# Four partial-sum tables in two alternating scatter chains, joined by VectorE and TensorE, in an attention and mixture-of-experts kernel

## The chip, the cores and the metric

The kernel runs on one core of one Trainium2 chip. The metric is the device time of one execution in microseconds (us). Engines: TensorE (PE in the profile; PEld is its weight load), VectorE (DVE), ScalarE (ACT), GpSimd (POOL) and SyncE (SP), which here only issues DMA transfers.

## The reference

Four batches of 1024 tokens with 256 values each go through two residual blocks in float32. A is causal attention with 16 query heads of 128 and 4 key and value heads with rotary positions. F is a mixture of experts: sigmoid scores of 64 experts, the best 4 of 8 groups, the best 6 experts in them, weights normalized and times 2.5, at most 48 tokens per expert, each expert a gated layer of 96, and beside it one shared expert of the same shape.

```python
x = x + layernorm(A(layernorm(x)))
x = x + layernorm(F(layernorm(x)))
# F: y = segment_sum(out[expert, slot] * weight, token); return y + shared(x)
```

## The kernel before

`attention` runs from the start to about 1780 us and also does the routing of the first seven of eight groups of 512 tokens (a "quad"); `last_quad` does the last quad and the shared expert; `experts` (L1626 on) takes the experts in 32 pairs and then finishes the output. The change is mostly in `experts`.

**Tables.** The sum over the experts of a token is kept in HBM, in partial-sum tables of 4144 rows (4096 tokens and 48 rows for padding) of 1 KB. All three are parts of one tensor `sums`. The shared expert is written to table 0 beforehand and the others start at zero: `attention` writes zeros to table 1 and copies them to table 2 at its step 40 (L1096). GpSimd adds a pair's 128 result rows to the tables by an indirect DMA with addition (a "scatter"); the even expert's 64 rows and the odd expert's 64 rows go to different tables, because one token may be in both. An accumulating DMA reads and writes back, so two scatters that can touch one table must not be in flight together; each waits for the landing of the one before in its chain.

**The chains before.** `in_third_table(j)` is true for every third pair up to the 27th. The other pairs form chain 0 (`added[0]`, tables 0 and 1, 23 scatters). The nine third pairs form chain 1 (`added[1]`): both of their halves go to table 2, so each is two scatters (`scatter_half`, L1732), one for each expert of the pair, the other's rows being sent out of bounds.

**Turns.** TensorE runs 35 turns. Turn s transposes the gathered tokens of pair s (L1876), does gate and up of pair s-1 (L1888), transposes the hidden values of pair s-2 (L1896) and does down of pair s-3 (L1903). ScalarE copies and applies tanh, VectorE multiplies in `hidden(s-1)` and weights the odd expert's rows in `odd(s-3)` (L1779), after which the pair's scatter may be issued. GpSimd's queue is in order: the gather of pair j+6, then the scatter of pair j (and one half of a third pair). The ring of gathered pairs has eight places, the ring of results `y` four.

**The finish.** The 32 token tiles are taken in eight units of four tiles (128 x 1024 values, 512 KB). SyncE loads table 2 into `m2` (L1705) when chain 1 has landed, and tables 0 and 1 into `m0` and `m1` (L1711) when chain 0 has. Then, for each unit: GpSimd adds m2 to m0 (L1751), VectorE adds m1 (L1796), takes mean and variance (L1798, L1803), ScalarE the root (L1857), VectorE seven small operations for the reciprocal root with one Newton step and the shift (L1807 to L1813), ScalarE normalizes (L1866), and VectorE (L1792) or for three of the units GpSimd (L1756) adds the residual `x1`. SyncE stores the unit (L1715). The x1 rows, 4 MB, are loaded at the seventh pair (L1700).

## Time and profile before

| | |
|---|---|
| median of three runs | 2067.99 us (2067.24 to 2068.68) |
| the profiled execution's own time | 2069.03 us |
| its span, first to last instruction | 2067.2 us |
| busy: TensorE, VectorE, ScalarE, GpSimd | 1869.7, 1348.5, 1155.7, 1303.5 us |
| mean granted TensorE clock | 0.942 of 2.4 GHz |
| expert turns, first TensorE to last TensorE instruction | 1847.8 to about 1977.5 us |
| last scatter issued, landed | 1995.1, 1998.9 us |
| loads of tables 0 and 1 issued, first addition | from 1998.9, 2004.4 us |
| last residual addition begins | 2062.6 us |

Times within the trace are microseconds from the start of the span. A busy time counts an engine's instructions, not its waits or issues; what an engine waited for is inferred from semaphore events.

### The profile page before, as it was taken

The numbers are of one execution on the slowest core, as the hardware profiler recorded it, in microseconds if no ns is written. First come the engines' busy times: TensorE is split into PE (matmuls) and PEld (weight loads), VectorE is DVE, ScalarE is ACT, GpSimd is POOL, SyncE is SP. The second block draws the span as 40 slices with busy tenths as digits, with TensorE's granted clock in tenths as the row PEclk, the third lists the DMA queues.
The fourth block names the chain that finished last, engine by engine and source line by source line (L and its number), as shares of the span: only waits on it lengthen the run. The fifth ranks groups of instructions, "written<-read, shape, count | busy, mean of one in ns | idle before, by whom it ended". The sixth has DMA issues, their size and how long they took to land. (4 is left out here: it accounts for less than half of the span.)

```text
span 2067.2 us, 34272 instructions
## 1 busy us (share of the span) xinstructions
PE 1869.7 (90%) x11782; PEld 1554.9 (75%) x11782; DVE 1348.5 (65%) x3198; ACT 1155.7 (56%) x2632; POOL 1303.5 (63%) x1057
## 2 busy tenths in 40 slices
PE   5999999999999999999999999999999999776820
PEld 4888888888888888888888888888888887442310
DVE  5566666667767677767767667766676678641228
ACT  3656666666666655656666556566656555232313
POOL 5758575767766666767585758576666654226843
PEclk8999999999999999999999999999999999895555
DMA  5003000001110101000200000010001000586374
GB/s 179 14 26 104 6 22 6 22 6 32 47 52 6 42 6 27 2 26 32 67 12 16 32 6 27 6 52 27 32 6 42 14 4 27 218 322 198 58 201 143
DMA packets 74233, 111.77 MB, mean 54 GB/s; under 512 B 10790, under 2 KB 54772, under 8 KB 72928
## 3 DMA queue, kind: packets, MB, share of 16 engines
q1 hardware_dynamic: 61040, 88.42, 12.8%
q0 software_dynamic: 8544, 12.73, 2.7%
q10 hardware_dynamic: 4480, 8.44, 1.2%
q8 instruction: 97, 1.59, 0.3%
q14 instruction: 72, 0.59, 0.1%
HBM read 81.90 MB, written 35.47 MB: 57 GB/s over the span
## 5 line engine op out<-in xcount | busy, mean ns | idle before, releaser
L561 PE MATMUL s_ps<-kT,q 128*128 128x512 f32 (+3 forms) x2304 | 584.4, 372 | 13.9 <-POOL q L1135 7.7
L824 DVE TENSOR_TENSOR pT<-t_ps,pT 128x512 fp32r<-128x512 f32 (+3 forms) x768 | 401.2, 550 | 191.4 <-ACT pT L969 190.1
L811 DVE TENSOR_REDUCE neg_max<-s_ps 128x1 f32<-128x640 f32 (+7 forms) x512 | 384.9, 752 | 111.3 <-PE s_ps L561 104.4
L561 PEld LDWEIGHTS s_ps<-kT,q 128*128 128x128 f32 x2304 | 408.4, 192 | 61.7 <-ACT probs L958 11.6
L586 PE MATMUL av_ps<-pT,v 128*128 128x512 f32 x1728 | 442.5, 400 | 2.7 <-DVE pT L824 2.7
L1120 POOL TENSOR_TENSOR k_roped<-raw,sinT 64x512 f32<-64x512 f32 x316 | 407.3, 1289 | 24.3
L969 ACT ACTIVATE pT<-t_ps 128x512 fp32r<-128x512 f32 (+3 forms) x768 | 348.7, 490 | 130.2 <-PE t_ps L571 125.3
L958 ACT ACTIVATE probs<-s_ps,neg_max 128x640 f32<-128x640 f32 (+7 forms) x512 | 381.9, 746 | 63.4 <-DVE neg_max L811 61.1
L586 PEld LDWEIGHTS av_ps<-pT,v 128*128 128x128 f32 x1728 | 311.7, 189 | 67.5 <-DVE pT L824 7.8
L571 PE MATMUL t_ps<-k_ident,probs 128*128 128x128 f32 x2304 | 340.1, 274 | 11.6 <-DVE pT L824 5.9
L1117 POOL TENSOR_TENSOR k_roped<-raw,cosT 128x512 f32<-128x512 f32 x158 | 204.7, 1296 | 219.5 <-ACT raw L930 200.8
L571 PEld LDWEIGHTS t_ps<-k_ident,probs 128*128 128x128 f32 x2304 | 263.3, 140 | 37.3 <-ACT probs L958 12.7
L598 PE MATMUL misc_ps<-w_o,avT 128*128 128x256 f32 x1536 | 237.9, 290 | 15.5 <-DVE y L856 8.1
L598 PEld LDWEIGHTS misc_ps<-w_o,avT 128*128 128x128 f32 x1536 | 205.0, 189 | 33.4 <-ACT raw L930 12.9
L856 DVE SCALAR_TENSOR_TENSOR y<-misc_ps,inv_sum,y 128x256 f32<-128x256 f32 x448 | 215.0, 480 | 14.1 <-PE misc_ps L598 6.1
L1122 POOL TENSOR_TENSOR raw<-k_roped 128x512 f32<-128x512 f32 x158 | 202.9, 1284 | 12.4
L518 PE MATMUL misc_ps<-xT,w_q 128*128 128x256 f32 x1524 | 204.2, 283 | 1.8 <-DVE y L856 1.8
L518 PEld LDWEIGHTS misc_ps<-xT,w_q 128*128 128x128 f32 x1524 | 194.7, 190 | 3.7 <-DVE y L856 2.4
L829 DVE TENSOR_TENSOR avT<-av_ps,avT 128x512 fp32r<-128x512 f32 x128 | 88.6, 692 | 135.6 <-ACT avT L976 135.4
L976 ACT ACTIVATE avT<-av_ps 128x512 fp32r<-128x512 f32 x128 | 76.3, 596 | 161.1 <-PE av_ps L586 159.1
L939 ACT ACTIVATE q<-raw 128x512 fp32r<-128x512 f32 x128 | 80.6, 630 | 151.1 <-POOL raw L1122 151.1
L1135 POOL TENSOR_TENSOR q<-raw,q 128x512 fp32r<-128x512 f32 x128 | 163.5, 1291 | 1.8 <-ACT q L939 1.8
(234 smaller groups left out, 1871.1 us busy)
## 6 DMA issues: line engine op xcount, KB each, us to landing
w_early<-in_expert_w SPq DMA_DIRECT2D x5, 2560.0 KB, 26.7
k_staged<-in_wpack SPq DMA_DIRECT2D x47, 256.0 KB, 2.9
k_staged<-in_wpack SPq DMA_DIRECT2D x16, 512.0 KB, 3.6
w_early<-sums SPq DMA_DIRECT2D x16, 512.0 KB, 8.5
e_w_late<-in_expert_w SPq DMA_DIRECT2D x3, 2560.0 KB, 21.5
sums<-sums ACTq DMA_DIRECT2D x1, 4144.0 KB, 15.6
k_xw<-in_x SPq DMA_DIRECT2D x4, 1024.0 KB, 5.8
k_xb<-in_x SPq DMA_DIRECT2D x4, 1024.0 KB, 5.1
```

What stands on the lines that cost most here:

```text
L518: last = pe.matmul(bank("q", macro, half)[:, h * 256:(h + 1) * 256], w_q[:, s, half, c, h * HD:(h + 1) * HD], pair(xT[:, b % 2, a, c], m), ...
L561: last = pe.matmul(out, q[:, macro % 2, a, h, int(big)], kT[:, g % 2, s, lo:hi], start=(n == 0), stop=(n == 2))
L571: last = pe.transpose(t_ps[n % 2][:, j * P:(j + 1) * P], probs[:, r % 3, (first + j) * P:(first + j + 1) * P], ident[:])
L586: last = pe.matmul(av_ps[:], v[:, g % 2, a, j], pT[:, s, part_slot(p) + j], start=(j == 0 and n == 0), stop=(j == blocks - 1 and n == 2))
L598: last = pe.matmul(misc_ps[:, h * HID:(h + 1) * HID], avT[:, a, 2 * half + h], w_o[:, s, 2 * half + h], start=(n == 0), stop=(n == 2))
L811: dve.reduce_max(neg_max[:, r % 16:r % 16 + 1], s_ps[:, r % 2, 0:(row_tile(r) + 1) * P], AX.X, negate=True).then_inc(max_ready, 1)
L824: dve.tensor_tensor(lo, t_ps[n % 2][:, 0:count * P].rearrange("p (j n) -> p j n", n=P), hi.bitcast(F32), ALU.subtract).then_inc(t_lo, 1)
L856: last = dve.scalar_tensor_tensor(target[:, t], src, inv, y[:, t], ALU.mult, ALU.add)
L958: act.activation(probs[:, r % 3, 0:width], s_ps[:, r % 2, 0:width], ACT.Exp, bias=neg_max[:, r % 16:r % 16 + 1], accum_out=row_sum[:, r % ...
L969: act.activation(pT[:, 0, slot + first:slot + first + count, r % 4], t_ps[n % 2][:, 0:count * P].rearrange("p (j n) -> p j n", n=P), ACT.C ...
L1117: pool.tensor_tensor(shape(cosed), shape(raw[:, n % 2]), table(cosT, 0, P), ALU.mult).then_inc(cos_done, 1)
L1120: pool.tensor_tensor(shape(rope[64 - lo:128 - lo]), shape(raw[lo:hi, n % 2]), table(sinT, lo, hi), ALU.mult).then_inc(sin_done, 1)
```

## The change

There are four tables. For the first 28 pairs (`TURNS = 14`), even pairs go to chain 0 (tables 0 and 1) and odd pairs to chain 1 (tables 2 and 3), each pair as one scatter. The last four pairs all go to chain 0. `attention` copies zeros to table 3 as well. The index calculation in `last_quad` has six VectorE operations in place of ten.

Tables 2 and 3 are loaded (8 MB) when chain 1 has landed, into `m2` and `m3`. VectorE adds m3 to m2, two units in each of its turns s = 31 to 34, behind `hidden` and `odd` of the turn, waiting for the unit's loads. Tables 0 and 1 are loaded as before when chain 0 has landed, now into `m0` in the late weights' space and `m1`, which is m3's space, so each unit also waits for its joining.

In the finish GpSimd adds m2 to m0; TensorE then adds m0 and m1 by two float32 matmuls with the identity into each of two PSUM banks (four matmuls of 512 columns per unit); VectorE takes the statistics from PSUM, and ScalarE normalizes from PSUM into m0. The Newton step is gone: VectorE does one reciprocal, GpSimd the two small operations of the shift (`shift_of(u-1)`, queued behind its addition of unit u), and VectorE adds all residuals, that of unit u-1 queued between the statistics and the reciprocal of unit u.

Besides, some semaphores of `attention` are merged (`quad_mv`, `quad_rstd` in place of one for each of y and x1; `zeroed` becomes a link of the chain), with the same order of work, and SyncE waits at the end of `attention` for both zero copies. The diff without these, and without declarations:

```diff
@@ attention, last_quad @@
-                    act.dma_start(sums[2], sums[1]).then_inc(zeros_copied, 16)
+                    for n in (2, 3):
+                        act.dma_start(sums[n], sums[1]).then_inc(zeros_copied, 16)
...
-TURNS = 9
-
-
-def in_third_table(j):
-    return j % 3 == 2 and j < 3 * TURNS
+TURNS = 14
+
+
+def in_second(j):
+    return j % 2 == 1 and j < 2 * TURNS
 
 
 def scattered_earlier(j):
-    return sum((1 + in_third_table(i)) for i in range(j) if in_third_table(i) == in_third_table(j))
+    return sum(in_second(i) == in_second(j) for i in range(j))
...
-            third = slice(2, 3 * TURNS, 3)
+            second, first = slice(1, 2 * TURNS, 2), (slice(0, 2 * TURNS, 2), slice(2 * TURNS, EXPERTS // 2))
             for i in range(2):
-                half, other = slice(64 * i, 64 * i + 64), slice(64 - 64 * i, 128 - 64 * i)
-                target = index.to_third[:] if i else index.to_row[:, third]
-                dve.tensor_scalar(target[half], c_ps[1][half, third], -1.0, FAR + 2 * TABLE, ALU.mult, ALU.add).then_inc(index_done, 1)
-                dve.tensor_scalar(target[other], c_ps[1][other, third], 0.0, 2 * FAR, ALU.mult, ALU.add).then_inc(index_done, 1)
-                for cols in (slice(0, 3 * TURNS, 3), slice(1, 3 * TURNS, 3), slice(3 * TURNS, EXPERTS // 2)):
-                    dve.tensor_scalar(index.to_row[half, cols], c_ps[1][half, cols], -1.0, FAR + i * TABLE, ALU.mult, ALU.add).then_inc(index_done, 1)
+                half = slice(64 * i, 64 * i + 64)
+                for cols, table in ((second, 2 + i), (first[0], i), (first[1], i)):
+                    dve.tensor_scalar(index.to_row[half, cols], c_ps[1][half, cols], -1.0, FAR + table * TABLE, ALU.mult, ALU.add).then_inc(index_done, 1)
...
@@ experts @@
+        sum_ps = [t_ps, gu_ps, hT_ps, y_ps]
+
+        def summed_tile(u, t):
+            return sum_ps[u % 4][t // 2][:, (t % 2) * HID:(t % 2) * HID + HID]
...
-        x1, m2, m0 = (flat[:, i * SIZE:(i + 1) * SIZE].rearrange("p (t n) -> p t n", n=HID) for i in range(3))
-        m1 = w_late[:].rearrange("p e n -> p (e n)")[:, 0:SIZE].rearrange("p (t n) -> p t n", n=HID)
+        x1, m2, m3 = (flat[:, i * SIZE:(i + 1) * SIZE].rearrange("p (t n) -> p t n", n=HID) for i in range(3))
+        m0, m1 = w_late[:].rearrange("p e n -> p (e n)")[:, 0:SIZE].rearrange("p (t n) -> p t n", n=HID), m3
...
-            sp.wait_ge(y_ready, last_pair(1))
-            sp.wait_ge(added[1], 32 * TURNS)
+            sp.wait_ge(y_ready, last_pair(2))
+            sp.wait_ge(added[1], 16 * TURNS)
             for u in range(UNITS):
-                first = 2 * TABLE + u * UNIT * P
-                sp.dma_start(unit(m2, u), tiles(sums[first:first + UNIT * P])).then_inc(loaded[u], 16)
+                first = u * UNIT * P
+                for dst, table in ((m2, 2 * TABLE), (m3, 3 * TABLE)):
+                    sp.dma_start(unit(dst, u), tiles(sums[table + first:table + first + UNIT * P])).then_inc(loaded[u], 16)
             sp.wait_ge(y_ready, PAIRS)
             sp.wait_ge(added[0], 16 * (PAIRS - TURNS))
             for u in range(UNITS):
                 first = u * UNIT * P
+                sp.wait_ge(joined, u + 1)
                 for dst, table in ((m0, 0), (m1, TABLE)):
...
-                if in_third_table(j):
-                    scatter_half(j, 0)
-                else:
-                    scatter(j)
-                if j and in_third_table(j - 1):
-                    scatter_half(j - 1, 1)
+                pool.wait_ge(y_odd, j + 1)
+                if scattered_earlier(j):
+                    pool.wait_ge(added[in_second(j)], 16 * scattered_earlier(j))
+                pool.indirect_dma_start(sums, bass.IndirectOffsetOnAxis(to_row[:, j:j + 1], 0), y[:, j % Y_RING], None,
+                                        bounds_check=4 * TABLE - 1, oob_is_err=False, compute_op=ALU.add).then_inc(added[in_second(j)], 16)
+            link = Links(pool, pool_chain, 0, 0)
+
+            def shift_of(u):
+                pool.wait_ge(rstd_ready, u + 1)
+                if u >= 2:
+                    pool.wait_ge(normed, u - 1)
+                link(pool.tensor_tensor(centre[:, u % 2], mv[:, u % 2, :, 0], rstd[:, u % 2], ALU.mult))
+                pool.tensor_tensor(shift[:, u % 2], kept.shift[:, u * UNIT:(u + 1) * UNIT], centre[:, u % 2], ALU.subtract).then_inc(shift_ready, 1)
+
             for u in range(UNITS):
-                pool.wait_ge(loaded[u], 48)
-                pool.tensor_tensor(unit(m0, u), unit(m0, u), unit(m2, u), ALU.add).then_inc(summed, 1)
-                if u >= 2 and on_pool(u - 2):
-                    if u == 3:
-                        pool.wait_ge(x1_in, 16)
-                    pool.wait_ge(normed, u - 1)
-                    pool.tensor_tensor(unit(m0, u - 2), unit(m0, u - 2), unit(x1, u - 2), ALU.add).then_inc(done[1], 1)
-            for n, count in enumerate((PAIRS - TURNS, 2 * TURNS)):
+                pool.wait_ge(loaded[u], 64)
+                pool.tensor_tensor(unit(m0, u), unit(m0, u), unit(m2, u), ALU.add).then_inc(padded, 1)
+                if u:
+                    shift_of(u - 1)
+            shift_of(UNITS - 1)
+            for n, count in enumerate((PAIRS - TURNS, TURNS)):
...
+                first = 2 * (s - (PAIRS + 3 - UNITS // 2))
+                for u in range(max(first, 0), first + 2):
+                    dve.wait_ge(loaded[u], 32)
+                    dve.tensor_tensor(unit(m2, u), unit(m2, u), unit(m3, u), ALU.add).then_inc(joined, 1)
...
-                link(dve.tensor_tensor(unit(m0, u), unit(m0, u), unit(m1, u), ALU.add))
+                if u >= 2:
+                    dve.wait_ge(mv_ready, u - 1)
+                    dve.wait_ge(shift_ready, u - 1)
                 for t in range(UNIT):
-                    last = dve.bn_stats(stats[:, t], m0[:, u * UNIT + t])
+                    last = dve.bn_stats(stats[:, u % 2, t], summed_tile(u, t))
                 link(last)
-                if u >= 2:
-                    dve.wait_ge(normed, u - 1)
                 for t in range(UNIT):
-                    last = dve.bn_aggr(mv[:, u % 2, t], stats[:, t])
-                last.then_inc(var_ready, 1)
+                    last = dve.bn_aggr(mv[:, u % 2, t], stats[:, u % 2, t])
+                last.then_inc(mv_ready, 1)
+                if u:
+                    residual(u - 1)
                 dve.wait_ge(root_done, u + 1)
-                mean, var, r = mv[:, u % 2, :, 0], mv[:, u % 2, :, 1], rstd[:, u % 2]
-                link(dve.reciprocal(r, root[:, u % 2]))
-                link(dve.tensor_tensor(newton[:], r, r, ALU.mult))
-                link(dve.scalar_tensor_tensor(newton[:], var, EPS, newton[:], ALU.add, ALU.mult))
-                link(dve.tensor_scalar(newton[:], newton[:], -0.5, 1.5, ALU.mult, ALU.add))
-                link(dve.tensor_tensor(r, r, newton[:], ALU.mult))
-                link(dve.scalar_tensor_tensor(shift[:, u % 2], mean, -1.0, r, ALU.mult, ALU.mult))
-                dve.tensor_tensor(shift[:, u % 2], shift[:, u % 2], kept.shift[:, u * UNIT:(u + 1) * UNIT], ALU.add).then_inc(rstd_ready, 1)
-                if u and not on_pool(u - 1):
-                    residual(u - 1)
+                dve.reciprocal(rstd[:, u % 2], root[:, u % 2]).then_inc(rstd_ready, 1)
             residual(UNITS - 1)
...
-                act.wait_ge(rstd_ready, u + 1)
+                act.wait_ge(shift_ready, u + 1)
                 for t in range(UNIT):
-                    at = m0[:, u * UNIT + t]
-                    last = act.activation(at, at, ACT.Identity, bias=shift[:, u % 2, t:t + 1], scale=rstd[:, u % 2, t:t + 1])
+                    last = act.activation(m0[:, u * UNIT + t], summed_tile(u, t), ACT.Identity, bias=shift[:, u % 2, t:t + 1], scale=rstd[:, u % 2, t:t + 1])
...
+            for u in range(UNITS):
+                pe.wait_ge(padded, u + 1)
+                if u >= 4:
+                    pe.wait_ge(normed, u - 3)
+                for k in range(2):
+                    bank = sum_ps[u % 4][k][:]
+                    for n, table in enumerate((m0, m1)):
+                        half = unit(table, u)[:, 2 * k:2 * k + 2].rearrange("p t n -> p (t n)")
+                        last = pe.matmul(bank, ident[:], half, start=(n == 0), stop=(n == 1))
+                last.then_inc(summed, 1)
+
```

## Rows read from the trace of the kernel before

**Rows 1.** GpSimd's timeline, steady turns: start, length, instruction, idle before it and releaser.
```profile
1927.37 1.59 POOL L1724 DMA_INDIRECT sums<-k_xb,i_to_row  x1 [0.30 <-issue]
...
1931.14 1.08 POOL L1741 DMA_INDIRECT i_gathered<-rows,i_from_row  x1 [0.30 <-issue]
...
1939.07 1.59 POOL L1724 DMA_INDIRECT sums<-k_xb,i_to_row  x1 [0.30 <-issue]
```

**Rows 2.** TensorE's timeline: starts of turns 15, 23, 24 and 28.
```profile
1905.96 0.69 PE L1876 MATMUL e_t_ps<-k_ident,i_gathered 128*128 128x128 f32 x2
...
1937.61 0.69 PE L1876 MATMUL e_t_ps<-k_ident,i_gathered 128*128 128x128 f32 x2
...
1941.14 0.69 PE L1876 MATMUL e_t_ps<-k_ident,i_gathered 128*128 128x128 f32 x2
...
1957.52 0.44 PE L1876 MATMUL e_t_ps<-k_ident,i_gathered 128*128 128x128 f32 x2 [1.67 <-DMA i_gathered<-rows,i_from_row]
```

**Rows 3.** The chain that ended last, first scatters: start, us from issue to landing.
```profile
1856.59 8.17 DMA sums<-k_xb,i_to_row
...
1865.62 7.04 DMA sums<-k_xb,i_to_row
...
1885.22 11.45 DMA sums<-k_xb,i_to_row
```

**Rows 4.** The same chain, from the 28th pair's scatter to the final loads.
```profile
1972.22 3.59 DMA sums<-k_xb,i_to_row
...
1976.62 5.16 DMA sums<-k_xb,i_to_row
...
1982.59 7.26 DMA sums<-k_xb,i_to_row
...
1990.66 3.67 DMA sums<-k_xb,i_to_row
...
1998.92 0.36 SPq L1711
```

**Rows 5.** Windows, the final loads: us, busy time by engine, granted clock, DMA share, GB/s.
```profile
2001.00:2026.00 25.00, 0.00 (x0) 0.00 (x0) 17.45 (x44) 5.04 (x11) 13.03 (x6) 0.50 1.09 352
```

**Rows 6.** Timeline of the finish.
```profile
2004.44 2.33 POOL L1751 TENSOR_TENSOR w_early<-w_early 128x1024 f32<-128x1024 f32 x1 [7.73 <-DMA e_w_late<-sums]
...
2010.46 2.34 DVE L1808 TENSOR_TENSOR e_newton<-e_rstd 128x4 f32<-128x4 f32 x1
...
2056.94 1.41 DVE L1798 BATCH_NORM_STATS2 e_stats<-w_early 128x6 f32<-128x256 f32 x4
...
2059.12 0.18 DVE L1807 RECIPROCAL e_rstd<-e_root 128x4 f32<-128x4 f32 x1 [0.36 <-ACT e_root L1857]
...
2060.52 2.07 ACT L1866 ACTIVATE w_early<-w_early,e_shift,e_rstd 128x256 f32<-128x256 f32 x4 [1.43 <-DVE e_shift L1813]
2062.63 1.23 DVE L1792 TENSOR_TENSOR w_early<-w_early 128x1024 f32<-128x1024 f32 x1 [1.01 <-ACT w_early L1866]
```

**Rows 7.** GpSimd's timeline: a small operation in `last_quad`.
```profile
1792.90 0.20 POOL L244 TENSOR_TENSOR k_work<-k_x_mv,k_x_rstd 128x4 f32<-128x4 f32 x1
```

**Rows 8.** One line's instructions, `odd`: count, shortest, median, longest ns.
```profile
L1779 DVE TENSOR_SCALAR k_xb<-e_y_ps,i_gathered x32: 488/490/493, 1855.3 to 1978.7; 64x256 f32<-64x256 f32 x32
```

**Rows 9.** TensorE's timeline, shared expert: two float32 matmuls of 512 columns each row.
```profile
1781.54 3.32 PE L1357 MATMUL r_gate<-k_staged,k_roped 128*96 128x512 f32 x4 [1.96 <-PEq L290]
...
1805.59 1.88 PE L1357 MATMUL r_gate<-r_xs,k_roped 128*96 128x512 f32 x4
1807.31 1.88 PE L1357 MATMUL r_up<-r_xs,k_roped 128*96 128x512 f32 x4
```

**Rows 10.** Windows of TensorE: us, busy, granted clock, DMA share, GB/s.
```profile
1784.00:1785.00 1.00, 1.00 (x3) 0.83 1.00 401
...
1958.00:1960.00 2.00, 2.00 (x13) 0.61 0.69 109
```

**Rows 11.** One line's instructions, the first gate matmuls, two records per matmul.
```profile
L1357 PE MATMUL r_gate<-k_staged,k_roped x4: 684/1061/1137, 1781.5 to 1784.2; 128*96 128x512 f32 x4
```

More of the change, by code:

```diff
@@ L357, in attention @@
         passed, copied, weight_done, weight_out = sem("passed"), sem("copied"), sem("weight_done"), sem("weight_out")
-        y_mv, x1_mv, x_mv, y_rstd, x1_rstd, x_rstd = (sem(n) for n in ("y_mv", "x1_mv", "x_mv", "y_rstd", "x1_rstd", "x_rstd"))
+        quad_mv, x_mv, quad_rstd, x_rstd = (sem(n) for n in ("quad_mv", "x_mv", "quad_rstd", "x_rstd"))
         score_done, biased_done, penalty_done, masked, picked_done, product_done, total_done = (
@@ L472, in _ @@
             sp.wait_ge(weight_out, 32 * (QUADS - 2))
-            sp.wait_ge(zeros_copied, 16)
+            sp.wait_ge(zeros_copied, 32)
         @block.tensor
@@ L696, in quad_stats @@
                 b, half = divmod(n, 2)
-                src, mv, mv_done, read = (xw, kept.y_mv, y_mv, y_rstd) if kind == "y" else (xb, kept.x1_mv, x1_mv, x1_rstd)
+                src, mv, turn = (xw, kept.y_mv, 2 * n) if kind == "y" else (xb, kept.x1_mv, 2 * n + 1)
                 if i == 0:
@@ L709, in quad_stats @@
                 else:
-                    if n:
-                        dve.wait_ge(read, n)
+                    if turn >= 2:
+                        dve.wait_ge(quad_rstd, turn - 1)
                     for k in range(4):
                         last = dve.bn_aggr(mv[:, k], kept.stats[:, k])
-                    last.then_inc(mv_done, 1)
+                    last.then_inc(quad_mv, 1)
             def add_residual(n, i):
                 if i == 0:
-                    dve.wait_ge(y_rstd, n + 1)
+                    dve.wait_ge(quad_rstd, 2 * n + 1)
                     dve.wait_ge(xb_in, 16 * (n // 2 + 1))
@@ L1658, in experts @@
         hT_ready, hT_read = sem("hT_ready"), sem("hT_read")
-        y_ready, y_even, y_odd = sem("y_ready"), sem("y_even"), sem("y_odd")
-        added = [sem(f"added{n}") for n in range(2)]
+        y_ready, y_even, y_odd, padded = sem("y_ready"), sem("y_even"), sem("y_odd"), sem("padded")
+        added, joined = [sem(f"added{n}") for n in range(2)], sem("joined")
         x1_in = sem("x1_in")
         loaded = [sem(f"loaded{u}") for u in range(UNITS)]
-        summed, var_ready, root_done, rstd_ready = (sem(n) for n in ("summed", "var_ready", "root_done", "rstd_ready"))
-        normed, done, stored = sem("normed"), [sem(f"done{n}") for n in range(2)], sem("stored")
+        summed, mv_ready, root_done, rstd_ready, shift_ready = (sem(n) for n in ("summed", "mv_ready", "root_done", "rstd_ready", "shift_ready"))
+        normed, done, stored = sem("normed"), sem("done"), sem("stored")
+        pool_chain = sem("pool_chain")
+        sum_ps = [t_ps, gu_ps, hT_ps, y_ps]
+        def summed_tile(u, t):
+            return sum_ps[u % 4][t // 2][:, (t % 2) * HID:(t % 2) * HID + HID]
         block = ctx.enter_context(nc.Block())
@@ L1676, in landed @@
         def landed(j):
-            return added[in_third_table(j)], 16 * (scattered_earlier(j) + 1 + in_third_table(j))
+            return added[in_second(j)], 16 * (scattered_earlier(j) + 1)
         def weights(e):
@@ L1686, in unit @@
             return a[:, u * UNIT:(u + 1) * UNIT]
-        def on_pool(u):
-            return u % 2 == 1 and u + 1 < UNITS
-        def finished(u):
-            return done[on_pool(u)], sum(on_pool(i) == on_pool(u) for i in range(u + 1))
         @block.sync
@@ L1712, in _ @@
             for u in range(UNITS):
-                sp.wait_ge(*finished(u))
+                sp.wait_ge(done, u + 1)
                 b, t = divmod(u * UNIT, NT)
@@ L1719, in _ @@
         def _(pool):
-            def scatter(j):
-                pool.wait_ge(y_odd, j + 1)
-                if j:
-                    pool.wait_ge(added[0], 16 * scattered_earlier(j))
-                pool.indirect_dma_start(sums, bass.IndirectOffsetOnAxis(to_row[:, j:j + 1], 0), y[:, j % Y_RING], None,
-                                        bounds_check=3 * TABLE - 1, oob_is_err=False, compute_op=ALU.add).then_inc(added[0], 16)
-            def scatter_half(j, i):
-                to = index.to_third[:, j // 3:j // 3 + 1] if i else to_row[:, j:j + 1]
-                pool.wait_ge(y_odd, j + 1)
-                if scattered_earlier(j) + i:
-                    pool.wait_ge(added[1], 16 * (scattered_earlier(j) + i))
-                pool.indirect_dma_start(sums, bass.IndirectOffsetOnAxis(to, 0), y[:, j % Y_RING], None,
-                                        bounds_check=3 * TABLE - 1, oob_is_err=False, compute_op=ALU.add).then_inc(added[1], 16)
             for j in range(PAIRS):
@@ L1855, in root_of @@
             def root_of(u):
-                act.wait_ge(var_ready, u + 1)
+                act.wait_ge(mv_ready, u + 1)
+                if u >= 2:
+                    act.wait_ge(rstd_ready, u - 1)
                 act.activation(root[:, u % 2], mv[:, u % 2, :, 1], ACT.Sqrt, bias=eps[:]).then_inc(root_done, 1)
@@ L1926, in build @@
         shared_in = ctx.enter_context(nc.semaphore("shared_in"))
-        attention(nc, args, x, wpack, x1_rows, rows, [sums[n * TABLE:(n + 1) * TABLE] for n in range(3)], x2t_rows, kept, shared_in)
+        attention(nc, args, x, wpack, x1_rows, rows, [sums[n * TABLE:(n + 1) * TABLE] for n in range(4)], x2t_rows, kept, shared_in)
         index = Index(lambda name, shape, dt=F32: ctx.enter_context(nc.sbuf_tensor("i_" + name, shape, dt)))
```

26 lines of the change are left out of this document (12 added, 14 removed).

## The prediction

> **What bounds the kernel now.** I read the page first. TensorE is busy 1869.7 of 2067.2 us, but that is attention, where the change adds only zero copies. So the question is the last 220 us, for which I read the chain that ended last, then the timelines of GpSimd and TensorE there, and the windows. Three stretches have three different limits.
>
> *The turns, 1848 to 1972.* In the steady part GpSimd never waits: between instructions it idles only 0.30 us of its own issue time. Two scatters three pairs apart start at 1927.37 and 1939.07, so three pairs take 11.70 us. That is four scatters (a third pair needs two) of 1.59 + 0.30 and three gathers of 1.08 + 0.30, or 3.90 us per pair [rows 1]. TensorE needs less: two turns without a wait start 3.53 us apart at the half clock (1.2 GHz) [rows 2]. Before 1900 the limit is different: scatters of chain 0 take 8.17, 7.04 and 11.45 us to land beside the loads of expert weights and of x1 [rows 3], and the in-order GpSimd queue, gathers included, stands behind them.
>
> *The tail, 1972.2 to 1998.9.* The 28th pair's scatter is issued at 1972.22, the four others follow each other's landings in chain 0, and the final loads are issued at 1998.92, which is 26.7 us later. Alone a scatter lands in 3.6 to 3.7 us, beside the table 2 loads in 5.16 and 7.26, and 0.8 us lie between a landing and the next issue [rows 4].
>
> *The finish, 1998.9 to 2067.2, 68.3 us.* GpSimd starts its first addition 5.5 us after the first load is issued. The loads run at 352 GB/s with the DMA share full [rows 5], so 1 MB of a unit takes 3.0 us, but units leave only every 7.3 us: the last VectorE operations begin at 2062.63 after eight units from 2004.44 [rows 6]. VectorE holds the chain. An operation on 128x4 values that elsewhere takes 0.16 to 0.20 takes 2.34 us when it lies under a GpSimd addition of the same length [rows 6, 7].
>
> **Part 1, one scatter per pair and four tables.** In the turns GpSimd then has one scatter and one gather, 1.89 + 1.38 = 3.27 us per pair, below TensorE's 3.53. So TensorE at the half clock becomes the limit, with no waits to hide: 3.54 us per pair, 0.36 less than before. The bound below is 3.27, if the clock rises in part. A chain has 7.1 us between its issues, more than the 3.7 of a landing, so it never holds the queue there.
>
> The start changes more. With two chains the second scatter no longer waits for the first to land: it goes at about 1859.9 in place of 1865.6, the eighth gather after it at 1861.8 in place of 1867.5. Carrying this forward pair by pair with the landings of [rows 3] (8 us beside the weights, 4 us between as alone, 11 beside x1, whose load also moves 4 us earlier) I get gathers at 1867.5, 1870.8, 1875.3, 1878.6, 1881.9, 1886.9 and 1894, and turn 15 begins at about 1898.1 in place of 1905.96 [rows 2], 7.9 us early. The 28th pair is done in turn 30: 1898.1 + 15 x 3.54 = 1951.2 is its start, + 3.54 for the turn, + 1.2 for ScalarE's and VectorE's halves and the issue, gives its scatter at 1956.2 to 1956.5. Before it was 1972.2: **-15.7 us**. The bounds are 1954 (GpSimd's pace) and 1960 (half the start's gain lost).
>
> **Part 2, the tail with 8 MB of loads and the joins.** It costs. Call the issue of the 8 MB L'; it follows the landing of the 28th pair, 3.8 us after its scatter. Loaded units come at L' + 5.5 and then every 3.0, the last at L' + 26.5, and nearly every scatter of the tail lies beside them. VectorE's queue is in order, so the joins also hold `hidden` and `odd` of the next turns, and for these TensorE and the scatters wait. The scatter of the 29th pair goes at L' - 0.3 and lands at L' + 7. Joins of units 0 and 1 end at L' + 9.7 (the unit at 8.5, a VectorE addition 1.2 [rows 6]); then the 30th pair's results and scatter at L' + 11, landed at 18.3 by the 7.26 of [rows 4]; the 31st at 19, landed at 26.3; the 32nd at 27, landed at L' + 30.8, where the loads are over. The joins are done by L' + 27.7, so the chain ends last. The final loads start 3.8 + 30.9 = 34.7 us after the 28th pair's scatter in place of 26.7: **+8.0 us**. With 5.2 per landing it would be L' + 28; with the 11.45 of the x1 load instead of 7.26 L' + 35: -3 and +4 us.
>
> **Part 3, the finish.** The final loads are again 8 MB, so the first addition is again 5.5 us after their issue and the padded unit 2.34 later. Per unit VectorE loses one addition (1.2), the Newton step and the slow small operations; TensorE gets four float32 matmuls of 512 columns. No such sum stands in the trace; nearest are the shared expert's gate and up, two such matmuls each: 1.72 us start to start at the full clock, 3.3 at the half one [rows 9]. So 3.44 or 6.7 us per unit. GpSimd's two small operations take 0.2 each [rows 7], statistics from PSUM 1.41 to 1.9 (between the 1.41 from SBUF [rows 6] and the 0.49 per tile of `odd`, which reads PSUM [rows 8]; I take 1.5, since it is the same operation).
>
> What limits is a loop: addition of unit u, TensorE's sum, statistics and aggregate, residual u-1, reciprocal, shift of u, and only then GpSimd adds unit u+2. At the full clock this is 2.34 + 3.7 for the sum with its last record's length + 1.9 for statistics and aggregate (the reciprocal starts 2.2 after the statistics, with ScalarE's root between [rows 6]) + 1.2 + 0.2 + 0.8 for the shift with its waits, 10.2 us for two units, 5.1 per unit. The first unit is padded 7.85 after the issue, the second 3.0 later, the eighth 3 x 10.2 after the second and 2.4 more for a first sum at the half clock, its sum 3.7 later: 39.7 after the first. The last statistics, residual of unit 7, reciprocal, shift, normalizing (2.07) and residual (1.2) are 1.9 + 1.2 + 0.2 + 0.8 + 2.1 + 1.2 and some waits, 7.6; store and end, as before, 3.3. Together 58.5 us.
>
> The clock. TensorE is cold before it. It rose 2.8 us after the first of the 512-column matmuls (1781.54, window 1784 to 1785) [rows 9, 10], so it will rise in the first unit; in the loop TensorE then idles 1.6 us in each 5.1. In the turns the clock fell within 2.5 us after an idle of 1.67 us (turn 28, window 1958 to 1960) [rows 2, 10], though smaller matmuls surrounded it. I therefore add 2 us for partial falls: 60.5 in place of 68.3, **-7.8 us**. Always cold, TensorE alone takes 8 x 6.9 (6.7 and a wait) = 55 us after the first padded unit: 7.85 + 55 + 7.6 + 3.3 = 73.8, or +5.5.
>
> The Trainium skill, page "TensorE: Matmul & The Clock Gate", section "A second HAM failure mode: psum-queue depth-cycling", describes a kernel whose TensorE idles briefly between groups of matmuls while it cycles PSUM banks, often enough that its clock keeps going back and forth. By that rule the finish would lie between my two cases; by the dense matmuls of the shared expert alone it would be the 58.5. No row before shows this loop.
>
> **Edits at nothing.** The second zero copy at step 40 lies in attention, where at that time no engine waited for a transfer; uncovered it would cost at most its 4 MB at 352 GB/s, 12 us. The four index operations removed end well before the weights' store that GpSimd waits for. The merged semaphores keep the order of work. SyncE's added waits for the joins are over before chain 0.
>
> **Sum.** -15.7 + 8.0 - 7.8 = -15.5: span 2051.7 in place of 2067.2. The profiled execution took 2069.03 and the median is 2067.99, 0.8 over the span, so 2052.5 us.
>
> **Rivals.** *Cold finish (no change):* TensorE's idles between units keep it at 1.2 GHz all through, and it limits at 6.9 per unit. With the other terms: -15.7 + 8.0 + 5.5 = -2.2, 2065.8 us. For it speaks that the turns run almost entirely at the half clock though TensorE is busy nearly without a break; against it that 512-column matmuls raised the clock each time. 7%.
>
> *Partly cold:* the clock goes back and forth, about 5.8 us per unit: 2058 us. 20%.
>
> *TensorE's sum dearer than its columns (slower):* if a matmul record of the sum takes at the half clock what the first gate records take each as a whole, 1.06 us [rows 11], eight of them make 8.5 us per unit; the finish is 7.85 + 68 + 7.6 + 3.3 = 86.8, +18.5, and the kernel is 10.8 slower, 2078.8 us. It is slower by over 0.2% from 7.6 us per unit on. The start-to-start times, which are shorter, speak against it. 6%.
>
> *Joins and loads hide better, or the turns speed up:* the clock rises in the turns now that TensorE has no waits, GpSimd's 3.27 becomes the limit, and scatters land in 5.2: 15.7 + 2.2 and 8.0 - 3 give 2047.3. 15%.
>
> *The change doesn't shorten the turns:* if y's ring or the landings hold the two chains, only the start's and the finish's gains stay: about 2058. 5%, with partly cold in effect.
>
> **The numbers.** The forecast case has 47%. The range of 2045 to 2064 leaves out the cold and the slower rival, about 13%, and a little more. Within 0.2% (about what a measurement tells from no change) means 2063.9 to 2072.1. Faster 0.86, same 0.08, slower 0.06.
>
> **What the trace after would show.** GpSimd's scatters some 3.5 us apart with TensorE's turns back to back; turn 15 near 1898 and the 28th pair's scatter near 1956; joins in VectorE's timeline that begin on a load's landing; landings of 5 to 8 us in the tail and the last loads near 1991; 512-column matmuls at the clock 1.00 after the first unit and 5 us between units. The prediction is wrong if the tail's landings are far over 7.3, if the clock stays at 0.50 in the finish, or if the turns keep 3.9 us.

## The result and the profile after

The changed kernel takes 2050.24 us (median of 4 runs, 2049.09 to 2051.49) against 2068.16 for the kernel before: ratio 0.9915, 95% interval 0.9901 to 0.9929. It is 17.9 us faster; the forecast was 15.5. In a later group of runs the same kernel gave 0.9902 (0.9887 to 0.9918). The profiled span is 2048.4 us.

The first section of the page after, which answers to the busy times in the table of before:

```profile
PE 1895.5 (93%) x11846; PEld 1566.2 (76%) x11846; DVE 1330.8 (65%) x3149; ACT 1154.0 (56%) x2632; POOL 1284.4 (63%) x1061
```

TensorE is busy 26 us more and the kernel is shorter: the sum of two tables has gone to an engine that stood idle there. The three stretches, by the two traces:

| | before | after | forecast |
|---|---|---|---|
| turn 15 of TensorE begins | 1905.96 | 1898.64 | 1898.1 |
| 28th pair's scatter issued | 1972.2 | 1953.3 | 1956.5 |
| from there to the final loads | 26.7 | 36.9 | 34.7 |
| final loads to the end | 68.3 | 58.2 | 60.5 |

*The turns.* GpSimd's timeline after, for [rows 1]; the same columns:

```profile
1921.77 1.60 POOL L1729 DMA_INDIRECT sums<-k_xb,i_to_row  x1 [0.59 <-issue]
1923.67 1.03 POOL L1724 DMA_INDIRECT i_gathered<-rows,i_from_row  x1 [0.31 <-issue]
1925.30 1.60 POOL L1729 DMA_INDIRECT sums<-k_xb,i_to_row  x1 [0.60 <-issue]
...
1942.11 1.60 POOL L1729 DMA_INDIRECT sums<-k_xb,i_to_row  x1 [0.30 <-issue]
1944.02 1.03 POOL L1724 DMA_INDIRECT i_gathered<-rows,i_from_row  x1 [0.31 <-issue]
1945.36 1.60 POOL L1729 DMA_INDIRECT sums<-k_xb,i_to_row  x1 [0.30 <-issue]
...
1953.30 1.55 POOL L1729 DMA_INDIRECT sums<-k_xb,i_to_row  x1 [1.22 <-DMA sums<-k_xb,i_to_row]
```

Read the distance of two scatters and the idle before them. At 1925 it is 3.53 us with 0.60 of idle, so GpSimd waits a little for each pair's results; at 1945 it is 3.25 us with the bare 0.30 of issue, so GpSimd is the limit. The last row is the 28th pair's scatter, which waited for a landing. TensorE's timeline, turns 13, 15, 22, 23, 25, 26 and 27, says why the distance shrank, for [rows 2]:

```profile
1891.57 0.69 PE L1863 MATMUL e_t_ps<-k_ident,i_gathered 128*128 128x128 f32 x2 [1.05 <-DMA i_gathered<-rows,i_from_row]
...
1898.64 0.69 PE L1863 MATMUL e_t_ps<-k_ident,i_gathered 128*128 128x128 f32 x2
...
1923.40 0.69 PE L1863 MATMUL e_t_ps<-k_ident,i_gathered 128*128 128x128 f32 x2
...
1926.93 0.69 PE L1863 MATMUL e_t_ps<-k_ident,i_gathered 128*128 128x128 f32 x2
...
1932.74 0.44 PE L1863 MATMUL e_t_ps<-k_ident,i_gathered 128*128 128x128 f32 x2
...
1934.74 0.44 PE L1863 MATMUL e_t_ps<-k_ident,i_gathered 128*128 128x128 f32 x2
...
1937.27 0.44 PE L1863 MATMUL e_t_ps<-k_ident,i_gathered 128*128 128x128 f32 x2 [0.46 <-DMA i_gathered<-rows,i_from_row]
```

Turns are 3.53 us apart at 1.2 GHz until 1931, then 2.0 us at 2.4 GHz until the gathers that have landed are used up and TensorE waits. Windows of TensorE show the clock (us, busy time with the number of rows, granted clock, DMA share, GB/s):

```profile
1912.00:1914.00 2.00, 2.00 (x10) 0.50 0.35 40
...
1936.00:1938.00 2.00, 1.54 (x11) 1.00 0.37 70
```

*The tail.* The chain that ended last, for [rows 4], and in the second block VectorE's timeline:

```profile
1953.30 3.64 DMA sums<-k_xb,i_to_row
...
1957.01 0.37 SPq L1702
...
1969.43 8.11 DMA sums<-k_xb,i_to_row
...
1978.35 6.84 DMA sums<-k_xb,i_to_row
...
1986.00 4.10 DMA sums<-k_xb,i_to_row
...
1990.16 0.36 SPq L1709
```

```profile
1963.34 1.23 DVE L1779 TENSOR_TENSOR w_early<-w_early 128x1024 f32<-128x1024 f32 x1 [8.13 <-DMA w_early<-sums]
1966.35 1.23 DVE L1779 TENSOR_TENSOR w_early<-w_early 128x1024 f32<-128x1024 f32 x1 [1.78 <-DMA w_early<-sums]
1967.61 0.25 DVE L1757 SCALAR_TENSOR_TENSOR k_xw<-k_xw,e_gu_ps 128x96 f32<-128x96 f32 x1
1967.90 0.25 DVE L1761 SCALAR_TENSOR_TENSOR k_xw<-k_xw,e_gu_ps 128x96 f32<-128x96 f32 x1
1968.18 0.49 DVE L1768 TENSOR_SCALAR k_xb<-e_y_ps,i_gathered 64x256 f32<-64x256 f32 x1
1969.37 1.22 DVE L1779 TENSOR_TENSOR w_early<-w_early 128x1024 f32<-128x1024 f32 x1 [0.69 <-DMA w_early<-sums]
```

VectorE stands 8.1 us in front of a join that waits for its loads; only behind the second join come the hidden values of the 32nd pair (L1757, L1761) and the odd half (L1768) of the 30th, and GpSimd idles 11.60 us for VectorE before the 30th pair's scatter.

*The finish.* GpSimd's timeline, for [rows 6]: the additions of the third, fifth and seventh unit, and before the last of them the small operation of the shift, which waits for VectorE's reciprocal:

```profile
2007.04 2.34 POOL L1742 TENSOR_TENSOR e_w_late<-e_w_late,w_early 128x1024 f32<-128x1024 f32 x1
...
2018.41 2.34 POOL L1742 TENSOR_TENSOR e_w_late<-e_w_late,w_early 128x1024 f32<-128x1024 f32 x1
...
2027.66 0.20 POOL L1737 TENSOR_TENSOR e_centre<-e_mv,e_rstd 128x4 f32<-128x4 f32 x1 [2.88 <-DVE e_rstd L1801]
...
2028.09 2.34 POOL L1742 TENSOR_TENSOR e_w_late<-e_w_late,w_early 128x1024 f32<-128x1024 f32 x1
```

From the fifth to the seventh unit it is 9.68 us from start to start. TensorE's timeline, rows of the first, third and fifth sums:

```profile
1998.04 2.08 PE L1912 MATMUL e_t_ps<-e_w_late,k_ident 128*128 128x512 f32 x2 [27.48 <-POOL e_w_late L1742]
...
2003.09 1.02 PE L1912 MATMUL e_t_ps<-w_early,k_ident 128*128 128x512 f32 x2
...
2009.43 1.88 PE L1912 MATMUL e_hT_ps<-e_w_late,k_ident 128*128 128x512 f32 x2 [1.89 <-POOL e_w_late L1742]
...
2020.80 1.12 PE L1912 MATMUL e_t_ps<-e_w_late,k_ident 128*128 128x512 f32 x2 [2.54 <-POOL e_w_late L1742]
2021.77 1.02 PE L1912 MATMUL e_t_ps<-w_early,k_ident 128*128 128x512 f32 x2
```

A matmul takes 1.02 us with 0.86 between starts at 2.4 GHz, and about 1.9 with 1.7 between starts at 1.2 GHz. The first sum (6.1 us) and the third (5.4) ran partly at the half clock, the others took 3.6 to 3.7. The third sum, 1.7 us longer than the 3.7 of the others behind an idle, made the distance from the third unit's addition to the fifth's 11.37 us, 1.7 more than the next 9.68: what TensorE's sum loses, the additions lose too.

### The profile page after: what moved, and what is told of

Its sections match the earlier page's. It is cut to its first block and busy times, and to the rows that moved or that the text cites. A ratio compares the mean times of both kernels' runs of the same rounds, so it can differ in the third digit from the quotient of the medians.

```text
span 2048.4 us, 34361 instructions
## 1 busy us (share of the span) xinstructions
PE 1895.5 (93%) x11846; PEld 1566.2 (76%) x11846; DVE 1330.8 (65%) x3149; ACT 1154.0 (56%) x2632; POOL 1284.4 (63%) x1061
## 5 line engine op out<-in xcount | busy, mean ns | idle before, releaser
L561 PEld LDWEIGHTS s_ps<-kT,q 128*128 128x128 f32 x2304 | 408.3, 192 | 61.6 <-ACT probs L958 11.6
L571 PE MATMUL t_ps<-k_ident,probs 128*128 128x128 f32 x2304 | 340.1, 274 | 11.6 <-DVE pT L824 7.9
L598 PE MATMUL misc_ps<-w_o,avT 128*128 128x256 f32 x1536 | 237.9, 291 | 15.5 <-DVE y L856 8.1
L1123 POOL TENSOR_TENSOR raw<-k_roped 128x512 f32<-128x512 f32 x158 | 202.8, 1283 | 12.4
```

Source lines behind the costliest of these rows:

```text
L561: last = pe.matmul(out, q[:, macro % 2, a, h, int(big)], kT[:, g % 2, s, lo:hi], start=(n == 0), stop=(n == 2))
L571: last = pe.transpose(t_ps[n % 2][:, j * P:(j + 1) * P], probs[:, r % 3, (first + j) * P:(first + j + 1) * P], ident[:])
L598: last = pe.matmul(misc_ps[:, h * HID:(h + 1) * HID], avT[:, a, 2 * half + h], w_o[:, s, 2 * half + h], start=(n == 0), stop=(n == 2))
```

## The experiments

Twelve runs follow, in three groups, eleven of changed versions and one of the changed kernel again; each group has its own runs of the kernel before, to which the ratios refer. A 95% interval is about 0.15% to each side, 3 us. Theory: the change is three separate terms (turns, tail, finish), with VectorE's in-order queue in the tail and a loop through GpSimd's queue in the finish as the two costs that it still has. The rivals stand in the expectations. What is said of a single stretch is read from one profiled execution of each kernel.

### One part alone

`old_finish` keeps tables, chains and joins and has the old finish with its Newton step and residuals; the diff shows its core against the changed kernel. `new_finish_only` has the same lines the other way round, against the kernel before, on its three tables and old chains.

```diff
-                pool.tensor_tensor(unit(m0, u), unit(m0, u), unit(m2, u), ALU.add).then_inc(padded, 1)
+                pool.tensor_tensor(unit(m0, u), unit(m0, u), unit(m2, u), ALU.add).then_inc(summed, 1)
...
-                    last = dve.bn_stats(stats[:, u % 2, t], summed_tile(u, t))
+                link(dve.tensor_tensor(unit(m0, u), unit(m0, u), unit(m1, u), ALU.add))
+                for t in range(UNIT):
+                    last = dve.bn_stats(stats[:, t], m0[:, u * UNIT + t])
...
-                        last = pe.matmul(bank, ident[:], half, start=(n == 0), stop=(n == 1))
```

> Four tables, two chains and the joins as in the changed kernel, but the finish of the kernel before (GpSimd adds m2, VectorE adds m1 and does the Newton step, no TensorE sum). Theory of three separate terms (turns -18.9 us, tail +10.2, finish -10.1, as the two traces give them): the span is 2067.2 - 18.9 + 10.2 = 2058.5 us, final loads issued near 1990 and the finish 68 us long. Rival, the terms depend on each other (the finish was long before only because it came behind a chain without joins and a late table 2): the finish is already near 58 us here and the span near 2049.

> Three tables and the chains of the kernel before, with the new finish (TensorE sums m0 and m1 in PSUM, one reciprocal, GpSimd the shift). Theory of separate terms: the finish takes 58 us instead of 68, span 2057 us, and the turns and tail stay as before (28th pair's scatter near 1972, final loads near 1999). Rival, the finish is fast only with TensorE still warm or with the early joins: 63 us or more, span over 2062.

Measured: `old_finish` 2059.72 us, ratio 0.9961 (0.9947 to 0.9975), span 2057.9, `new_finish_only` 2056.61 us, 0.9950 (0.9933 to 0.9966), span 2057.3. SyncE's timeline has the first of the final loads of `old_finish`, and then of `new_finish_only`:

```profile
1989.72 0.36 SPq L1709 DMA_DIRECT2D e_w_late<-sums  x1
```

```profile
1999.30 0.36 SPq L1711 DMA_DIRECT2D w_early<-sums  x1
```

The old finish takes 2057.9 - 1989.7 = 68.2 us behind the new tail, the new finish 2057.3 - 1999.3 = 58.0 behind the old one: the lengths of before and after to within 0.2 us. The savings of 0.39% and 0.50% add to 0.89%, where the change has 0.85 and, in the later group, 0.98. The terms are separate, and new chains with joins bring less than half of it.

### The joins behind the last turn

```diff
-                first = 2 * (s - (PAIRS + 3 - UNITS // 2))
-                for u in range(max(first, 0), first + 2):
-                    dve.wait_ge(loaded[u], 32)
-                    dve.tensor_tensor(unit(m2, u), unit(m2, u), unit(m3, u), ALU.add).then_inc(joined, 1)
+            for u in range(UNITS):
+                dve.wait_ge(loaded[u], 32)
+                dve.tensor_tensor(unit(m2, u), unit(m2, u), unit(m3, u), ALU.add).then_inc(joined, 1)
```

> The changed kernel with all eight joins behind the last turn of VectorE instead of two in each of the last four turns. Theory 1 (the joins hold the results of the last three pairs: the 30th pair's scatter stands 11.6 us behind VectorE): the scatters go out right behind each other's landings, the last lands about 29 us after the issue of the 8 MB instead of 33, and the span is about 4 us shorter, 2044 to 2045. Theory 2 (landings beside 8 MB of loads set the tail, whoever waits in front of them): landings of 8 us and more one behind the other, less than 1 us gained.

Measured: 2043.76 us, ratio 0.9886 (0.9870 to 0.9903), span 2043.8. GpSimd's timeline, the scatters of the 30th and 31st pair:

```profile
1963.54 1.55 POOL L1729 DMA_INDIRECT sums<-k_xb,i_to_row  x1 [4.79 <-DMA sums<-k_xb,i_to_row]
1971.23 2.21 POOL L1729 DMA_INDIRECT sums<-k_xb,i_to_row  x1 [6.14 <-DMA sums<-k_xb,i_to_row]
```

Both now idle for the landing before them and not for VectorE. The final loads go at 1986.53, 28.4 us after the first of the 8 MB (1958.16) where the change needs 33.1. The VectorE queue was worth 4.8 us; theory 2 falls. What is left, 28.4, is still the chain, by the chain that ended last: the landings of the 30th, 31st and 32nd pair took 6.88, 7.57 and 6.85 us one behind the other. The 8 MB would now allow little more: VectorE's last join, which waits for the last of them, began at 1986.8.

### GpSimd's additions one unit further ahead

```diff
-                if u:
-                    shift_of(u - 1)
+                if u >= 2:
+                    shift_of(u - 2)
+            shift_of(UNITS - 2)
             shift_of(UNITS - 1)
```

> The changed kernel with the shift of unit u-2, not u-1, behind GpSimd's addition of unit u. Theory 1 (the finish is a loop through GpSimd's queue: addition of unit u+2 stands behind the shift of unit u, 9.7 us for two units): the additions run ahead with the loads, and VectorE with ScalarE's normalizing sets about 4.3 us per unit, finish 3 to 4 us shorter, span about 2045. Theory 2 (TensorE's sum and its clock, or VectorE's own work, set the pace already): under 1 us of gain; if TensorE falls to the half clock in the longer idles, slower.

Measured: 2042.28 us, ratio 0.9879 (0.9862 to 0.9895), span 2043.4. GpSimd's additions of two neighbouring units:

```profile
2016.99 2.35 POOL L1742 TENSOR_TENSOR e_w_late<-e_w_late,w_early 128x1024 f32<-128x1024 f32 x1
...
2021.02 2.34 POOL L1742 TENSOR_TENSOR e_w_late<-e_w_late,w_early 128x1024 f32<-128x1024 f32 x1
```

4.03 us per unit instead of 4.84, and the finish takes 51.3 us instead of 58.2. (In this profile the final loads came 2.0 us later than in the change's, so the span is 5.0 shorter.) The loop through the queue order is shown; theory 2 falls. The gain, 6.9, is larger than the 3 to 4 expected. About 5 of it is the pace; the rest is most likely the third unit, whose addition no longer stands behind the first shift and whose sum, without an idle before it, ran at the full clock (1.7 us). No run separates the two.

### The sum done twice

```diff
-                    for n, table in enumerate((m0, m1)):
+                    for n, table in enumerate((m0, m1, m0, m1)):
...
-                        last = pe.matmul(bank, ident[:], half, start=(n == 0), stop=(n == 1))
+                        last = pe.matmul(bank, ident[:], half, start=(n % 2 == 0), stop=(n % 2 == 1))
```

> The changed kernel with TensorE's sum of every unit done twice (eight float32 matmuls of 512 columns per unit, the second four overwriting the first). Theory 1 (TensorE's sum lies in the loop of the finish, with GpSimd's addition, the statistics and the shift): 3.44 us more in each two-unit loop makes 6.9 us per unit, at the full clock, and TensorE has no idle; finish about 15 us longer than the changed kernel's 58, span near 2063. Theory 2 (VectorE and GpSimd alone set the pace and the sum lies beside them): under 3 us more.

Measured, in a single execution: 2067.36 us, span 2065.6, final loads at 1989.86, so the finish takes 75.7 us, 17.5 more. TensorE's timeline:

```profile
2026.90 1.02 PE L1912 MATMUL e_y_ps<-w_early,k_ident 128*128 128x512 f32 x2
2027.76 1.02 PE L1912 MATMUL e_t_ps<-e_w_late,k_ident 128*128 128x512 f32 x2
```

A unit takes 6.87 us, eight starts 0.86 apart, with no idle left. So theory 2's under 3 us is refuted, but the run doesn't tell the theories apart as it was meant to: with 6.87 us of matmuls per unit TensorE is the limit by itself, which it would also be if its sum lay beside a loop of 4.84. That the sum lies in the loop is shown by the change's own third sum, above. The run also prices the rival of the cold finish: a TensorE at half speed all through would have done 6.9 us per unit, and given back nearly the whole gain of the change.

### The clock of the first sums

`warm_start` has ten more matmuls of 512 columns between the last join and the first unit.

```diff
+            pe.wait_ge(joined, UNITS)
+            for _ in range(10):
+                pe.matmul(y_ps[1][:], ident[:], unit(m2, 0)[:, 0:2].rearrange("p t n -> p (t n)"), start=True, stop=True)
```

> The changed kernel with ten more matmuls of 512 columns on TensorE (their results are overwritten by the fourth unit's sum) between the last join and the first unit of the finish. Theory 1 (the first sums run at 1.2 GHz because TensorE stood idle before): the clock is 1.00 when the first unit is padded, its sum takes 3.6 us instead of 6.1, and the finish is about 2.5 us shorter, up to 4 if the third unit's sum is warm too; span 2044 to 2046. Theory 2 (the first two units are hidden behind the loads): no change within 1 us.

Measured: 2049.61 us, ratio 0.9907 (0.9890 to 0.9923), span 2047.7, final loads at 1991.95. TensorE's timeline:

```profile
1988.30 11.91 PE L1906 MATMUL e_y_ps<-w_early,k_ident 128*128 128x512 f32 x20 [16.09 <-DVE w_early L1779]
2000.04 1.02 PE L1915 MATMUL e_t_ps<-e_w_late,k_ident 128*128 128x512 f32 x2
```

The first sum is at the full clock and the finish takes 55.8 us instead of 58.2, as theory 1 has it. The further gain that it gave for a warm third sum did not come: that sum was warm, but the seventh was not (its first row took 1.81 us), so the fall of the clock had only moved. The median does not show it: its interval and the change's overlap almost wholly. So 2.5 us in one trace, not more than that.

### The improvements together

`joins_pad` has the late joins and the further additions, `all_three` the ten matmuls as well.

> The joins behind the last turn and the additions of GpSimd one unit further ahead, together. If the tail and the finish are separate stretches, the two gains add up: 4.6 + 5.0 us by the profiled spans, span near 2039. If the earlier tail only moves a limit of the loads into the finish, the sum is less than the larger one plus 2.

> The two together and the ten warming matmuls. If the first sum's half clock still lies on the path, 2 us or more below joins_pad, near 2037; if the loads now limit the first units, the same as joins_pad within 1 us.

Measured: `joins_pad` 2037.83 us, 0.9856 (0.9840 to 0.9873), `all_three` 2038.84 us, 0.9854 (0.9837 to 0.9870). The two gains add. The warming matmuls do not help, and their trace says why:

```profile
1988.73 11.44 PE L1906 MATMUL e_y_ps<-w_early,k_ident 128*128 128x512 f32 x20 [32.02 <-DVE w_early L1779]
2000.01 1.02 PE L1915 MATMUL e_t_ps<-e_w_late,k_ident 128*128 128x512 f32 x2
```

With the joins last they begin later against the first unit, which was ready at 1992.9, and stand 7 us in front of its sum. This profile is of the slowest of its four executions, and the medians differ by 1.0 us only, so the 7 us are not shown for the others.

### The load of x1

The start of the turns still collides with the 4 MB of x1. `x1_late` issues it at the 16th pair, `joins_pad_x1` has this with the late joins and additions, and `joins_pad_x1_warm` also four warming matmuls. `after_again` is the changed kernel in the same group.

```diff
-            sp.wait_ge(y_ready, last_pair(0))
+            sp.wait_ge(y_ready, 16)
```

> The changed kernel unchanged, so that the others of this group have it on the same chip. 2050 us, ratio 0.991 to 0.992 to the kernel before; final loads about 33 us after the first of the 8 MB, finish about 58 us.

> The changed kernel with the 4 MB of x1 loaded at the 16th pair instead of the 7th. Theory 1 (at the start the collision costs, because the gathers have no lead left: TensorE waited 3.09 and 1.05 us for gathers beside that load; at the 16th pair a gather is issued six pairs ahead and GpSimd has slack): turn 15 begins 3 to 4 us earlier, near 1895, and most of it stays to the end, span about 2045. Theory 2 (a load of 4 MB costs the chains the same wherever it is put): turn 15 is earlier, the 28th pair's scatter is not; the same within 1 us.

> The late joins, the additions further ahead, and x1 at the 16th pair. The gains are in three separate stretches, so they should add: 2038 us less what the late x1 load gives alone, about 2034.

> The same with four warming matmuls instead of the ten, which stood 7 us in front of the first sum when the joins came last. Theory 1 (they fill only the idle before the first unit and raise the clock): the first sum takes under 4 us instead of 5.3, 1 to 2 us less than the kernel without them. Theory 2 (the first units are covered by the loads): the same within 1 us.

Measured: `after_again` 2049.73 us, 0.9902 (0.9887 to 0.9918), its final loads 33.6 us after the first of the 8 MB and its finish 57.8 us; `x1_late` 2049.67 us, 0.9908 (0.9893 to 0.9923); `joins_pad_x1` 2036.53 us, 0.9841 (0.9827 to 0.9854); `joins_pad_x1_warm` 2037.67 us, 0.9851 (0.9836 to 0.9866). TensorE's timeline of `x1_late`, turns 15 and 19:

```profile
1891.24 0.44 PE L1863 MATMUL e_t_ps<-k_ident,i_gathered 128*128 128x128 f32 x2
...
1911.91 0.69 PE L1863 MATMUL e_t_ps<-k_ident,i_gathered 128*128 128x128 f32 x2 [6.93 <-DMA i_gathered<-rows,i_from_row]
```

Turn 15 begins 7.4 us earlier than in the change (1.0 of it lies before GpSimd's first gather), but TensorE then waits 6.93 us for one gather beside the load. The collision is moved and not avoided, as theory 2 has it. In this one profile the 28th pair's scatter came 3.3 us early all the same, with TensorE at the full clock for more of the turns; the medians give no difference. `joins_pad_x1` is the fastest version measured, 32 us below the kernel before and some 13 below the change, but it can't be told from `joins_pad`, whose interval overlaps. The four warming matmuls bring nothing that the medians show.

## Why the prediction was right

**The sum** of -15.5 came out as -18.8 by the spans (-17.9 by the medians). Direction and places of the three terms were right and the waits were mostly the ones named; each term was off by 2.2 to 3.2 us, two to the good and one to the bad, so the tail's extra cost brought the total nearer to the forecast.

**Part 1, turns: -15.7 forecast, -18.9 measured.** The start came out, turn 15 at 1898.64 for 1898.1, and the gathers carried forward from the landings were issued within 1.4 us of the forecast times. But turn 15 did not wait for its gather. What set it was turn 13, which waited for the gather issued at 1881.51; this took 10.0 us to land beside the load of x1, a wait that the forecast doesn't name, and two turns of 3.53 us followed. That the time agrees to 0.5 us is partly luck.

What was mis-sized is the steady part, 15 x 3.54 us with TensorE at the half clock throughout. TensorE did become the limit at 3.53 us, but at 1931 its clock rose, and from there GpSimd's 3.25 us set the pace up to the 26th pair's scatter at 1948.61. Then the gathers were over, and the 28th pair's scatter waited 1.22 us for the landing of the 26th's, in a chain that was said never to hold the queue. From the start of turn 15 to that scatter 54.7 us passed; 58.4 were forecast, of which the terms written down give only 57.8 (1951.2 + 3.54 + 1.2 is 1955.9 and not 1956.2 to 1956.5). The scatter at 1953.3 lies just outside the stated bounds of 1954 and 1960. That the clock fell again near 1945 cost nothing: in `after_again` it stayed at 2.4 GHz to the last turn, and the same stretch took 54.5 us. The rival "the turns speed up" (15%) is in part what happened.

**Part 2, tail: +8.0 forecast, +10.2 measured.** The mechanism was as forecast step by step: the 30th pair's scatter went 12.4 us after the issue of the 8 MB (forecast 11), held by VectorE's joins. The tail was 2.2 us dearer because of these 1.4 (the second join began at 9.3 and not 8.5, and 1.9 instead of 1.3 passed from its end to the scatter) and because that scatter landed in 8.11 us, not 7.26; 1.0 of this is its own issue, below. The two later landings (6.84 and 4.10 for 7.26 and 3.8) almost cancel. The forecast named VectorE's queue but drew no conclusion from it; `joins_last` shows that 4.8 us of the +10.2 were avoidable.

**Part 3, finish: -7.8 forecast, -10.1 measured.** The loop was right: 9.68 us for two units for 10.2, shown by `pad_ahead` and by the third sum's 1.7 us, which the additions lost too. The residual held the reciprocal for 1.0 us and the shift took 0.55, where the sum had 1.2 and 0.8. The statistics from PSUM cost 1.43 us, near the lower bound of 1.41. From the last statistics to the end of the last residual it was 6.8 us for 7.6. The 2 us added for a clock that falls were about right: it fell once, in the third sum, which took 5.4 us for 3.7. The Trainium skill's rule of a clock that goes back and forth (page "TensorE: Matmul & The Clock Gate", section "A second HAM failure mode: psum-queue depth-cycling") is borne out only in part, by one fall in the eight units, after an idle of 1.89 us; later idles of 1.95 and 2.54 us left the clock at 1.00, as these windows of the change show:

```profile
2012.00:2014.00 2.00, 2.00 (x5) 0.73 1.10 349
...
2020.00:2022.00 2.00, 1.20 (x3) 1.00 0.20 62
...
2028.00:2030.00 2.00, 0.53 (x2) 1.00 0.77 261
```

Which sum meets the fall differs from run to run: the third here, the fifth in `after_again` and `new_finish_only`, the seventh in `joins_last`, `warm_start` and `x1_late`, each time one only and after an idle of 1.87 to 1.89 us. In `pad_ahead`, where no idle between sums is over 0.33 us, it stayed at 1.00 from the second sum to the last. When the clock falls is not worked out here, and 2 us for it was a good guess.

**Other sums of the prediction.** The upper bound of the tail puts 11.45 us in place of 7.26 for one landing of the chain, not for all that lie beside the loads. The last rival keeps the gains of start and finish and the cost of the tail, -7.9 + 8.0 - 7.8, which gives 2060.3 us and not about 2058; the forecast doesn't hang on it.

**Edits at nothing** stayed at nothing: `experts` begins at 1847.26 after, 1847.8 before.

**Open:** how much of the turns' gain depends on when the clock rises; it rose at about 1931 and 1932 in the two profiles of this kernel, and the 28th pair's scatter came at 1953.3 and 1954.1. Nor does a run separate, in the turns, the second chain from the single scatter per pair: by the traces 7.3 us of the 18.9 were gained before turn 15 and 11.6 behind it.

## What to carry to other kernels

When a queue at its limit runs one operation more than needed per item, take that out, and ask at once which engine is next and what clock it has: here 3.90 us per pair became 3.53 while TensorE stood at the half clock, and only above it the queue's own 3.25. An addition put into "idle" turns of an in-order engine is not free if it waits for a transfer; everything queued behind waits too, so put it after the last item that others need. And a producer that queues the consumer's small step behind each item can be run one item further ahead, which was here worth at least as much as the late joins.

## What the runs showed of the hardware

A scatter's own issue on GpSimd takes 1.55 to 1.63 us, but 2.58 and 2.04 us where it began under a VectorE addition of two SBUF operands. GpSimd's timeline of the change:

```profile
1969.43 2.58 POOL L1729 DMA_INDIRECT sums<-k_xb,i_to_row  x1 [11.60 <-DVE k_xb L1768]
1978.35 1.55 POOL L1729 DMA_INDIRECT sums<-k_xb,i_to_row  x1 [6.33 <-DMA sums<-k_xb,i_to_row]
1986.00 2.04 POOL L1729 DMA_INDIRECT sums<-k_xb,i_to_row  x1 [6.09 <-DMA sums<-k_xb,i_to_row]
```

The join of 1969.37 had begun just before the first and ended at 1970.59, 1.16 us after its start; the scatter's issue is 1.03 longer. The second began before its join (1978.92) and lost nothing. The third began under the join of 1985.39 to 1986.61. The first and third issue ended 1.42 and 1.43 us after the addition did, and so did the 2.21 us one of `joins_last` (join 1970.79 to 1972.01, 1.43). However much of the addition was left, nearly the whole issue came behind it. The Trainium skill says that GpSimd and VectorE share a pair of SBUF ports and that whoever starts first gets it for the whole instruction, VectorE in a two-port mode or, against a GpSimd operation that reads SBUF, with two SBUF inputs; as what keeps GpSimd from writing DMA descriptors it names a two-port operation (page "SBUF — State Buffer", section "SBUF: two separate sides"). The traces agree that the first to start holds the other up; they show it for the issue of a scatter under a float32 addition with two SBUF inputs. Whether it is the scatter's indices or its descriptors that wait, no run here tells.

TensorE's clock stayed at 1.2 GHz (granted clock 0.50 in every window of 2 us) from the wait that ended at 1891.6 to 1930, though its timeline has no idle in between, and rose at about 1931 (0.71 in the window from 1930, 1.00 in the next) while its turns had the same matmuls of the same shapes. What released it, the traces don't show.
